# Reordering the third step of a gated attention and feed-forward block on one core: guess before the last norm, its numbers before the low values, keys before the mixing

## The reference, cut to what matters

```python
x = x + tanh(g_xattn) * xattn(layernorm(x), ctx)
x = x + tanh(g_ffn)   * ffn(layernorm(x))

# xattn: emb = layernorm(x) + ctx; q, k, v = emb @ wq + bq, emb @ wk + bk, emb @ wv + bv
#   ew = exp(w - max w), w = pos_bias inside a band of |i - j| < 64, 0 outside; ek = exp(k - max k)
#   y = sigmoid(q) * (ew @ (ek * v)) / (ew @ ek)
#   a = layernorm(y @ wo + bo + emb) * gamma + beta
#   out = layernorm(relu(a @ w1 + b1) @ w2 + b2 + a) * gamma + beta
# ffn: xr, xk = mixes of x with the row before it (mu_r, mu_k)
#   out = sigmoid(xr @ W_r.T) * (square(relu(xk @ W_k.T)) @ W_v.T)
```

## Time and profile before

| | us |
|---|---|
| median of 3 runs | 457.03 (455.7 to 459.4) |
| the profiled execution, its own time | 455.05 |
| its span, first to last instruction | 453.2 |
| TensorE (PE) busy | 433.6 (96%) |
| VectorE (DVE) busy | 377.4 (83%) |
| GpSimd (POOL) busy | 289.4 (64%) |
| ScalarE (ACT) busy | 286.5 (63%) |

### The profile page before, as it was taken

How to read it: one execution, slowest core, us unless ns; L and a number is a source line. 1 busy time by engine, 2 the same in 40 slices (tenths; PEclk the granted TensorE clock), 3 DMA queues, 4 the chain that set the end, 5 groups by cost and what they waited for, 6 DMA issues and landing times.

```text
span 453.2 us, 8152 instructions
## 1 busy us (share of the span) xinstructions
PE 433.6 (96%) x2892; PEld 393.5 (87%) x2892; DVE 377.4 (83%) x770; ACT 286.5 (63%) x453; POOL 289.4 (64%) x229
## 2 busy tenths in 40 slices
PE   8979989999699999999999999999999999999985
PEld 7869789999589898998889888998889998998975
DVE  5998859987698979799798979799788877678876
ACT  3682653836677487745967487745966387629373
POOL 3476837573678557894778647894777543773632
PEclk9999999999899999999999999999999999999999
DMA  8840420443215650438315660435212330011002
GB/s 280 279 139 3 129 81 2 131 125 83 93 67 165 190 144 8 139 113 226 93 49 161 190 149 25 140 103 188 95 46 98 100 122 19 1 48 47 3 0 94
DMA packets 43497, 47.23 MB, mean 104 GB/s; under 512 B 8512, under 2 KB 39744, under 8 KB 43456
## 3 DMA queue, kind: packets, MB, share of 16 engines
q1 hardware_dynamic: 42368, 45.13, 32.7%
q10 hardware_dynamic: 1088, 1.57, 1.0%
HBM read 30.76 MB, written 15.93 MB: 103 GB/s over the span
## 4 chain that ended last, share of the span: by engine, by line
POOL 35%; issue 26%; PE 16%; DVE 10%; ACT 9%; DMA 2%; SPq 0%; POOLq 0%; DVEq 0%; ACTq 0%
PE ps L1835 15%; POOL ev_lo L242 6%; POOL ek_lo L242 5%; POOL x_beta L650 3%; POOL emb L354 3%; POOL xk_lo L242 2%; POOL a_rows L650 2%; POOL rs_mid L630 2%; POOL rs_fin L630 2%; POOL nmr_fin L633 2%; POOL rs_ff L630 1%; DVE ps L978 1%; DVE xk L1061 1%; DVE xr L1061 1%; ACT ev_hi L1530 1%
## 5 line engine op out<-in xcount | busy, mean ns | idle before, releaser
L1835 PE MATMUL ps<-w_hi,hid_hi 128*128 128x256 f32 x248 | 61.2, 283 | 1.3 <-ACT hid_hi L1789 0.8
L1835 PE MATMUL ps<-w_lo,hid_hi 128*128 128x256 f32 x248 | 60.8, 281 | 0.0
L1616 ACT ACTIVATE hid_hi<-ps,b 128x512 fp32r<-128x512 f32 x60 | 37.7, 681 | 23.6 <-PE ps L1835 23.5
L242 POOL TENSOR_TENSOR ek_lo<-y,ek_hi 128x1024 fp32r<-128x1024 f32 x13 | 36.2, 2785 | 24.6 <-DVE xr L1061 17.8
L1835 PE MATMUL ps<-a_hi,w_hi 128*128 128x512 f32 x128 | 50.7, 396 | 0.0
L1835 PE MATMUL ps<-a_hi,w_lo 128*128 128x512 f32 x128 | 50.7, 396 | 0.0
L1835 PEld LDWEIGHTS ps<-w_hi,hid_hi 128*128 128x128 f32 x248 | 46.7, 188 | 2.2 <-issue 1.9
L1835 PEld LDWEIGHTS ps<-w_lo,hid_hi 128*128 128x128 f32 x248 | 46.7, 188 | 0.3
L1138 DVE SCALAR_TENSOR_TENSOR hid_lo<-ps,neg_b,hid 128x512 fp32r<-128x512 f32 x60 | 41.3, 737 | 3.2 <-ACT hid L1622 3.2
L242 POOL TENSOR_TENSOR ev_lo<-res,ev_hi 128x1024 fp32r<-128x1024 f32 x8 | 19.2, 2396 | 35.2 <-ACT ev_hi L1530 35.2
L1622 ACT ACTIVATE hid<-hid_hi,neg_b 128x512 f32<-128x512 f32 x60 | 40.0, 722 | 0.0
(11 more groups left out here) (286 smaller groups left out, 1394.4 us busy)
## 6 DMA issues: line engine op xcount, KB each, us to landing
x_in<-in_x SPq DMA_DIRECT2D x8, 512.0 KB, 4.8
emb<-in_ctx SPq DMA_DIRECT2D x8, 512.0 KB, 4.5
x_beta<-in_x SPq DMA_DIRECT2D x8, 512.0 KB, 4.3
out<-out_sb SPq DMA_DIRECT2D x7, 512.0 KB, 4.3
key_room<-norm SPq DMA_DIRECT2D x6, 512.0 KB, 2.6
y<-key_room SPq DMA_DIRECT2D x24, 128.0 KB, 2.9
fin_room<-xk SPq DMA_DIRECT2D x6, 512.0 KB, 2.6
out_sb<-fin_room SPq DMA_DIRECT2D x24, 128.0 KB, 3.0
```

What stands on the lines that cost most here:

```text
L242: eng.tensor_tensor(dst, src, f32(hi), ALU.subtract).then_inc(done, 1)
L1616: act.activation(tile(hi, b, T), bank(relu_pair(n, q), b), ACT.Relu, bias=b1[:, m:m + 1]).then_inc(hid_hi_done, 1)
L1835: return pe.matmul(o, s, m, start=start, stop=stop, skip_group_check=True)
```

## The change

It touches step 2 and the end of step 1, in three of the engines' lists. Nothing is added or taken away.

- POOL, end of `first_step`: the numbers of the norm "fin" of batch 0 come before `ev_low(d)`, not after.
- DVE: `turn_fin_squares(0)` moves from the end of step 1 into step 2, between the first and the second half of `inverse`. `key_max(3)` and `head_stats(4)` move from behind `mix_k(0)`, `mix_r(0)` to before them.
- ACT: `normalise("fin", 0)` moves from the end of step 1 to behind `guess(2)`; `sums_high(2, 1)` comes before `emb_high(3)`; `y_high(2)` comes before `turned_copy(0)`, `scaled_copies(0)`.
- Steps 3 to 7 keep their order.

```diff
@@ gpsimd, first_step
                 ek_low(pool, d)
                 stats("ff", b)
+                stats("fin", b)
                 ev_low(d)
-                stats("fin", b)
@@ vector, first_step
                 hidden_low(i, 1)
                 normalise_fin(b)
-                turn_fin_squares(b)
@@ vector, step
                 inverse(i, 0)
+                if a == 0:
+                    turn_fin_squares(a)
                 inverse(i, 1)
                 sums_low(i, 1)
                 gate_inverse(i)
                 make_y(i)
+                if a == 0:
+                    key_max(d)
+                    head_stats(e)
                 mix_k(a)
                 mix_r(a)
                 if is_last(i):
                     last_step(i, p, a, b)
                     return
-                key_max(d)
-                if has(e):
-                    head_stats(e)
+                if a > 0:
+                    key_max(d)
+                    if has(e):
+                        head_stats(e)
                 turn_key_squares(d)
@@ scalar, first_step
                 ev_high(d)
-                normalise("fin", b, x1)
@@ scalar, step
                 guess(i)
+                if a == 0:
+                    normalise("fin", a, x1)
+                    sums_high(i, 1)
                 if has(d):
                     emb_high(d)
-                sums_high(i, 1)
+                if a > 0:
+                    sums_high(i, 1)
+                else:
+                    y_high(i)
                 turned_copy(a)
                 scaled_copies(a)
-                y_high(i)
+                if a > 0:
+                    y_high(i)
                 mixed_high(a)
                 mixed_r_high(a)
```

## The result

The changed kernel takes 457.66 us (median of 20 runs, 456.55 to 458.46), the kernel before 456.01 us (20 runs, 454.84 to 459.4). The ratio is 1.0029, with a 95% interval of 1.0018 to 1.0040: slower by 0.8 to 1.8 us. The profiled execution took 457.05 us with a span of 455.2, against 455.05 and 453.2 before. So the time is inside the forecast's range and close to its value, but that closeness is luck. The forecast was a shift of +0.4 us, and the shift measured is about +1.3 by the ratio. The 457.4 was built on a median of three runs, 457.03, which lies 1.0 us above the median of all 20, and that made up for the 0.9 us that the shift fell short.

The account below looks back on a forecast made before the run. PE, busy 96%, bounds the kernel. Terms -3.86 - 1.68 + 4.2 + 1.68, with +0.3 on PE, +0.4 on POOL, +0.5 less 0.2 on ACT, taken as +0.4: 455.45 profiled, 457.4 us median; range 454.0 to 460.6.

Parts of the forecast that it names:

- shift of +0.4 us: Whole kernel: the predicted net change, a loss of 0.4 us, with bounds +0.2 to +0.6; chance 0.64.
- The old stop would go (-3.86, -1.68): PE before the far sums' low part, steps 1 and 2: 3.86 us of waiting and 1.68 us of slow clock vanish.
- a cost that no row prices: DVE's norm tiles (L1039) beside POOL's ev_low: blocking costs between nothing and 2.3 us; taken as nothing.
- The port rival: L1039 waits for ev_low's end, PE stops 2.0 us at the sums: 459.4, or 461.1 with slow clock; chance 0.13.
- `ev_low` wasn't too late: Rival: POOL's ev_low comes over 1.2 us late and PE stops ahead of the sums, about 458.5; chance 0.06.
- no lead was kept: Rival, lead partly kept: the clock stays up after the new stop and PE sets the step, 455.7; chance 0.11.
- The new stop before wo's low part (+4.2): PE in step 2 stands from 125.4 to 129.6, 4.2 us, waiting for POOL's y_lo, which follows the mixes.
- The new stop's clock (+1.68): PE behind the new stop: falls to 1.2 GHz again, costing 1.68 us, with bounds 0 and 1.68.
- A shift made in step 2 stays: Later steps are unchanged and follow with the same shift; PE idles only 0.31 us in 51.39 there.
- Edits costed at nothing: Steps 1 and 2: emb_high and its low part hide behind PE; early y_high alone would save nothing.
- numbers before low values: POOL, end of step 1: norm numbers before ev_low let ACT and DVE start at 110.5, 2.0 us earlier.

Follow-up runs that it names:

- e8: The kernel before with a bench of DVE instructions, alone and beside POOL, behind its last store; its total of 470.7 us says nothing.
- e1_hold_low: The changed kernel with one wait more: POOL starts ev_low only after DVE's two tiles of the norm; 455.80 us, ratio 0.9983 to the kernel before.
- e2: The changed kernel with key_max and head_stats put back behind the mixes in step 2; 455.60 us, ratio 0.9989 to the kernel before.
- e6: The changed kernel with only y_low of step 2 moved ahead of POOL's wait for the mixes; 455.54 us, ratio 0.9997 to the kernel before.
- e3: The changed kernel with ev_low held back until DVE's tiles are through and the mixes ahead of key_max and head_stats; 453.59 us, ratio 0.9938.
- e7: e3 with y_high of step 2 put back behind turned_copy and scaled_copies; 453.87 us, ratio 0.9959 to the kernel before.
- e4: The changed kernel with POOL's edit undone, ev_low ahead of the norm's numbers again; 456.97 us, ratio 1.0023 to the kernel before.
- e9: e5 with key_max alone ahead of the mixes in step 2, head_stats staying behind them; 453.02 us, ratio 0.9935 to the kernel before.
- e5: e3 with y_low of step 2 moved ahead of POOL's wait for the end of mix_r; 453.57 us, ratio 0.9951 to the kernel before.

## Why the prediction was right and where it failed

**The old stop would go (-3.86, -1.68).** Half right. The stop shrank by 2.31 us and its slow stretch went, but 1.55 us stayed. The guess came first and its exponentials ran from 110.45; `sums_low` was then due at 115.4 and ran at 117.03. The step that failed is the one priced "a cost that no row prices", with "I take nothing". L1039 did wait for `ev_low`: 1.95 us of the 2.3 us that stood there as the upper bound, and more than the 1.5 us at which the text itself had this rival decide. The reason given was that two instructions of 256 elements in 0.73 us have the same pace per element as two-input ones of 512 in 1.42. e8 shows what was wrong with it: at 256 elements 276 of 409 ns are fixed, so a mean at one length says nothing on the pace. Two lengths were needed, and the trace of the kernel before had them. `key_max` ends with a tensor_scalar from SBUF on a single element (L851; count, then total us and mean ns of one):

```profile
L1039 DVE TENSOR_SCALAR norm<-x,rs_fin,nmr_fin 128x256 f32<-128x256 f32 x15 | 5.5, 410 | 4.3 <-POOL nmr_fin L633 4.3
L851 DVE TENSOR_SCALAR kbias<-neg_kmax,vec 128x1 f32<-128x1 f32 x16 | 3.6, 269 | 0.3
```

From these two, (410 - 269)/255 = 0.55 ns per element, half of the 1.0 of two-input instructions: the pace that e8 measured later, and with it the argument for "I take nothing" falls. The rule of the Trainium skill that the text set aside was the better evidence.

**The port rival, in its own numbers.** Tiles end at 113.5 (113.14), sums' stop 2.0 us (1.55), `keys` end at 122.7 (122.27), mixes at 129.1 (128.55). It had a chance of 0.13 and gave +2.4 us; measured was +1.3 by the ratio and +2.0 by the two profiled executions. This rival, not the forecast, is what happened. e1_hold_low is the forecast's world: with the blocking taken away the ratio was 0.9983 (0.9968 to 0.9998) where the forecast's shift of +0.4 would be 1.001. So without that blocking the change would have been no loss, and the forecast's small loss isn't borne out either; which of its terms hid that isn't shown. In e1's trace the transposes stand at 140.43, less the 0.55 us level with the 139.92 before, where the forecast had 140.2. Of the other rivals, `ev_low` wasn't too late (it ended at 112.66, and PE read it from 113.92 without a stop), and no lead was kept at 136.41.

**The new stop before wo's low part (+4.2).** Right in place, cause and size: 3.86 us, ended by POOL, which waited for the mixes, which stood behind `head_stats`, `key_max` and `keys`. The shares are another matter, and e2 and e6 give them: with the mixes first `y_low` starts 1.23 us earlier (127.39, not 128.62), so `head_stats` in front of them made 1.2 us of the stop, and the greater part, 2.7 us (e3), is POOL's wait for mixes that could not be earlier, which `y_low` doesn't need (e6). The sum of `key_max` and `head_stats`, 3.37 us, was met to the hundredth (122.47 to 125.84).

**The new stop's clock (+1.68).** Right: 0.66 from 130 to 135. Wo's low part to `ffn_r` took 131.02 to 136.41, 5.39 us, for the 5.44 of the forecast.

**A shift made in step 2 stays.** Right: 1.7 us at 141.63 and 2.0 at the end of the span.

**Edits costed at nothing.** `sums_high` before `emb_high` and the new place of `emb_low` hid as said; `y_high` first brought nothing that e7 can tell; numbers before low values brought nothing, which I had put at 2.0 us and e4 shows.

The range, 454.0 to 460.6, was wide: 20 runs of the changed kernel span 1.9 us, though those of the kernel before span 4.6.

## What to carry to other kernels

An instruction moved to an earlier time gets new neighbours: check which instruction of POOL is open in that stretch and can block it, not only what it waits for. Holding back the other engine by 1 us, with one wait more, can then be the cheaper order. And work put into an idle stretch of an engine must end with that stretch. Here the 1.75 us that DVE idled ahead of `key_max` cost nothing, since ACT's copies kept the mixes back until 124.58 (e2); `head_stats` ran beyond that, to 125.84, and held up mixes that were ready. Last, look at what a wait guards: the new stop hung on one wait placed ahead of an instruction that didn't need it. Taking it away wasn't the whole cure, since PE then stopped for 2.92 us at the next wait (e6).

## What the runs showed of the hardware that I had not expected

- A float32 tensor_scalar from SBUF costs 276 ns plus 0.52 ns per element with two per-partition scalars. At 256 elements it looks no faster than bn_stats (409 and 427 ns), and yet a POOL instruction of 2.34 us, begun 0.09 us earlier, holds it up to its end, while bn_stats passes beside.
- The clock doesn't follow from the length of a stop alone. Behind 1.55 us it stayed at 2.4 GHz in the changed kernel's profile (granted 1.00 from 120 to 125), behind 1.52 us in e2 it fell to 1.2 GHz for a while (0.73), and behind 1.84 us in e9 too (0.74 from 130 to 135). The other way round, it stayed at 2.4 GHz behind the 2.92 us of e6 (1.00), and fell behind the 2.54 us of e5 (0.51). Which stops cost the clock wasn't found out. The stretch behind the stop in e2:

```profile
120.00:125.00 5.00, 5.00 (x18) 3.91 (x16) 1.17 (x3) 3.28 (x5) 0.75 (x1) 0.73 0.32 85
```
- The same kernel differs by this from execution to execution: of the changed kernel's 20, nine with a mean granted clock of 0.994 to 0.996 took 456.55 to 457.05 us, and eleven with 0.990 or 0.991 took 457.53 to 458.46. The middles of the two groups, 456.72 and 458.12, lie as far apart as the whole effect of the change.
